# A turn ahead of the values: the order of TensorE's work in a head of attention

## The chip, the cores and the metric

One core of a Trainium2 chip runs one program. The time is the device's, in microseconds (us), from three runs of the kernel; lower is better. The profile is one further execution.

## What is computed

Two layers on `x` of 4 batches, 512 rows and 256 columns. Each layer is a cross attention with 16 heads of width 16 and a feed-forward part, each added to `x` through a gate. The attention of the first layer, cut to what matters (the second has one mask for all heads in place of the bias for each):

```python
q = split_heads(query @ Wq.T + bq)
k = split_heads(key @ Wk.T + bk)
v = split_heads(value @ Wv.T + bv)
scores = jnp.einsum('bhqd,bhkd->bhqk', q, k) / jnp.sqrt(jnp.asarray(DH, q.dtype))
scores = scores + relative_bias
scores = jnp.where(key_padding_mask[:, None, None, :], scores, -jnp.inf)
attn = jax.nn.softmax(scores, axis=-1)
out = jnp.einsum('bhqk,bhkd->bhqd', attn, v)
```

The first layer's feed-forward part is an expert network chosen for each batch, the second's a mixture of eight experts with a shared one.

## The kernel before, in words

Each engine has its own instruction stream, written out by hand, and waits on semaphores. A layer's attention is one phase, `attention_phase`. It runs over 4 groups of heads (`hg`), in each over 4 batches (`b`), in each over 4 heads (`j`): 64 heads one after the other, numbered `n`. Below, a "batch" is four heads of one group, 16 of them in a layer.

A head of one batch has scores of 512 x 512, in four tiles of 128 queries by 512 keys. A tile goes through these stations:

- PE, `scores` (L601): one matmul into one of three PSUM banks. Tiles go out in pairs. After the first two heads the tiles of two heads alternate in `order`: (n,0), (n+1,0), (n,1), (n+1,1) and so on. A matmul may start once the tile three places before in the ring of banks has been read.
- DVE, `add_bias` (L686): adds bias or mask, keeps the row's minimum of the negative as `nmax`, writes the tile to SBUF (`s`, or the spare `xT` for every other pair of heads).
- POOL, `subtract_max` (L795), for 7 of 8 tiles, ACT (L740) for the eighth.
- PE, `turn` (L615): 32 transposes of 64 x 64 bring the head's four tiles into four other PSUM banks. It waits until all four tiles of the head are subtracted (`less_max`, `pool_less_max`), and until ACT has read the banks for the head before (`exp0`, `exp1`).
- ACT, `exps` (L745, and L753 in a batch's last head): the exponential, into `pT`.
- PE, `values` (L633): one key tile `kt` of all four heads of a batch; four calls, kt = 0 to 3, make the batch's output. It can start when the last head's exponentials are there. ACT's `keep_out` copies the finished output to `oT`; a batch later PE's `turn_out` (L643) turns it, and DVE divides by the sums.

So the values of a batch are computed during the four heads of the next batch, one call in each head. `scores` runs ahead of `turn` by two heads and more: `tiles_issued(n)` is 10 + 4n tiles (8 for n = 0), and `between(n)` says that head n issues two tiles (`early`) and two more (`late`). Behind a batch's values stands POOL's copy `keep_values` (L801), once a batch, ahead of the last three tiles of its part.

SP loads queries, keys and, in the first layer, a bias of 1 MB for each head. DVE waits for the bias (`bias_loaded`).

In a head PE issues: values, early scores, in a batch's first head the turned output, the turn, late scores. That is the loop `body` of the PE stream.

Of the kernel before, what the change touches and what calls it, by code (L numbers as in the profile page):

```python
# [31 lines left out]
HG = 4  # L32
# [410 lines left out]
def attention_phase(nc, sem, sb, at, dram, bias_dram, zeroed, tag):  # L443
# [28 lines left out]
    def groups(eng, body):  # L472

        for hg in range(GROUPS):
            body(hg, hg == 0, hg == GROUPS - 1)

    def before(hg, b):

        return (hg, b - 1) if b else (hg - 1, B - 1)
# [23 lines left out]
    def between(n):  # L503

        return (0, 6) if n == 0 else (2, 2)
# [23 lines left out]
    def ring_bank(place):  # L529

        return (0, 1, 7)[place % 3]

    def tiles_issued(n):

        return AHEAD + 4 * n + (2 if n else 0)

    def slot(b, j):

        return j + HG * (b % 2) if j < HG - 1 else j

    with nc.Block() as block:
# [44 lines left out]
        @block.tensor  # L586
        def _(pe):
            pe.nop().then_inc(scores_done, 32)

            def scores(u):  # L590

                for n, k in order[u:u + 2]:
                    hg, b, j = n // M, n % M // HG, n % HG
                    place = tile_place[at_order[n, k]]
                    loads = hg * 2 + b // 2 + 1 - (b % 2 if at.joint_load else 0)
                    if j == 0 and k == 0 and loads:
                        pe.wait_ge(qk_loaded[b % 2], loads * (16 * LOADS))
                    if place >= 3:
                        pe.wait_ge(*ring[place - 3])
                    rows = slice(j % 2 * HP, j % 2 * HP + KEPT)  # L600
                    nc.tensor.matmul(sb.ps[:, ring_bank(place), :],  # L601
                                     at.qs[rows, j // 2, b % 2, k * P:(k + 1) * P],
                                     at.ks[rows, j // 2, b % 2, :], start=True, stop=True).then_inc(scores_done, 1)

            def turn(hg, m):

                pe.wait_ge(less_max, act_upto[hg * M + m])
                pe.wait_ge(pool_less_max, pool_upto[hg * M + m])
                for kt in range(QT):
                    if kt % 2 == 0:  # L610
                        pe.wait_ge(exp1 if kt else exp0, hg * M + m + 1)
                    for qt in range(QT):
                        for r in range(2):
                            rows, col = slice(r * HP, (r + 1) * HP), (kt % 2 * QT + qt) * HP
                            last = nc.tensor.transpose(sb.ps[:, 2 + kt // 2 * 2 + r, col:col + HP],  # L615
                                                       at.s[m % 4][rows, qt, kt * P:(kt + 1) * P],
                                                       sb.ident[rows, rows])
                    if kt % 2 == 1:
                        last.then_inc(turned, 1)

            def values(hg, b, kt):

                if kt == 0:
                    pe.wait_ge(exp_first, hg * B + b + 1)
                else:
                    pe.wait_ge(exp1 if kt >= 2 else exp0, hg * M + HG * b + HG + 1)
                if kt == 0:
                    pe.wait_ge(v_ready, hg * B + b + 1)
                    pe.wait_ge(out_kept, hg * B + b + 1)
                for j in range(HG):  # L630
                    pair = at.pT[:, slot(b, j), kt // 2 * 2:kt // 2 * 2 + 2, :].rearrange(
                        "p r (k t s) -> p k t r s", k=2, t=QT)
                    last = nc.tensor.matmul(sb.ps[VW * j:VW * (j + 1), 6, :], at.vq[:, b % 2, kt, j, :],  # L633
                                            pair[:, kt % 2, :, :, :], start=(kt == 0), stop=(kt == QT - 1))
                if kt == QT - 1:
                    last.then_inc(av_done, 1)

            def turn_out(hg, b):
                pe.wait_ge(out_kept, hg * B + b + 2)
                place = out_place[hg * B + b]  # L640
                pe.wait_ge(*ring[place - 3])
                for qt in range(QT):
                    last = nc.tensor.transpose(sb.ps[:, ring_bank(place), qt * P:(qt + 1) * P], at.oT[:, qt * P:(qt + 1) * P],  # L643
                                               sb.ident[:, :])
                last.then_inc(out_turned, 1)

            for u in range(0, AHEAD, 2):
                scores(u)

            def body(hg, first, last):  # L650
                for m in range(M):
                    b, j = m // HG, m % HG
                    u = tiles_issued(hg * M + m)
                    if not (first and b == 0):
                        values(*before(hg, b), j)
                    early, late = between(hg * M + m)
                    for i in range(0, early, 2) if u < len(order) else ():
                        scores(u + i)
                    if j == 0 and not (first and b < 2):
                        turn_out(*before(*before(hg, b)))  # L660
                    turn(hg, m)
                    for i in range(early, early + late, 2) if u + early < len(order) else ():
                        scores(u + i)
                if last:
                    turn_out(hg, B - 2)
                    for kt in range(QT):
                        values(hg, B - 1, kt)
                    turn_out(hg, B - 1)
            groups(pe, body)

        @block.vector
# [1640 lines left out]
```

## Time and profile before

| what | value |
|---|---|
| median of 3 runs | 944.98 us |
| lowest of them | 939.49 us |
| highest of them | 4893.35 us |
| the profiled execution's own time | 940.07 us |
| its span, first to last instruction | 938.3 us |
| mean granted TensorE clock | 0.975 |

The three runs are the first timings of the kernel; the highest stands alone. In the profile, attention takes two stretches of the span, from about 61 to 266 us and from about 415 to 616 us. The profile counts an engine as busy while an instruction that computes runs; the start of an instruction minus the start of the one before is what a step costs on an engine that never idles.

### The profile page before, as it was taken

What the parts mean: (1) busy time and instruction counts of PE and PEld (TensorE: products, weight loads), DVE (VectorE), ACT (ScalarE), POOL (GpSimd) and SP (SyncE); (2) the same over time, 40 slices, a digit from 0 to 9 for tenths busy, and PEclk for the clock granted to TensorE, in tenths of its full rate; (3) what the DMA queues carried; (4) which work ended last, traced back from release to release, by engine and by line L of the source; (5) the groups of instructions that cost most, each with busy time, mean ns of one, the idle gap of its engine ahead of it and who ended that gap; (6) DMA issues with size and microseconds to landing.
All of it is one profiled execution on the core that took longest, in us unless ns stands there. A gap on an engine that the chain in (4) does not pass through costs nothing. (4 is left out here: it accounts for less than half of the span.)

```text
span 938.3 us, 20996 instructions
## 1 busy us (share of the span) xinstructions
PE 895.9 (95%) x7733; PEld 555.0 (59%) x7734; DVE 563.9 (60%) x1659; ACT 452.2 (48%) x645; POOL 459.9 (49%) x648
## 2 busy tenths in 40 slices
PE   7889999999989999999999999997999899999998
PEld 2466555555567455556555555574555677777765
DVE  4558989899828334367999999757522222222226
ACT  2426767788745233346777777833111122323221
POOL 2017878888847600017888888741264022222224
PEclk9987999999999999986999999999999999999999
DMA  9853535453143331344242424033822021212216
GB/s 327 307 207 115 181 113 169 146 165 108 32 144 104 131 111 64 121 146 112 69 123 71 123 69 126 22 94 147 252 86 92 11 68 58 68 57 68 62 60 238
DMA packets 70372, 111.82 MB, mean 119 GB/s; under 512 B 17574, under 2 KB 41578, under 8 KB 68106
## 3 DMA queue, kind: packets, MB, share of 16 engines
q1 hardware_dynamic: 62458, 91.26, 31.6%
q0 software_dynamic: 3408, 9.38, 2.8%
q10 hardware_dynamic: 4416, 9.96, 2.8%
q8 instruction: 58, 0.95, 0.4%
q14 instruction: 32, 0.26, 0.1%
HBM read 76.99 MB, written 33.58 MB: 118 GB/s over the span
## 5 line engine op out<-in xcount | busy, mean ns | idle before, releaser
L745 ACT ACTIVATE pT<-ps 128x1024 f32<-128x1024 f32 x224 | 219.9, 1027 | 86.5 <-PE ps L615 86.4
L795 POOL TENSOR_SCALAR s<-s,nmax 128x512 f32<-128x512 f32 x218 | 148.5, 693 | 171.8 <-DVE nmax L686 168.1
L795 POOL TENSOR_SCALAR xT<-xT,nmax 128x512 f32<-128x512 f32 x224 | 153.2, 694 | 55.5 <-DVE nmax L686 55.4
L686 DVE CUSTOM_DVE_ANT_0 xT<-ps,bias 128x512 f32<-128x512 f32 x240 | 156.3, 688 | 23.8 <-PE ps L601 14.5
L686 DVE CUSTOM_DVE_ANT_0 s<-ps,bias 128x512 f32<-128x512 f32 x224 | 145.8, 688 | 11.8 <-PE ps L601 5.8
L601 PE MATMUL ps<-ks,qs 49*128 49x512 f32 (+1 forms) x512 | 140.8, 511 | 5.9 <-DVE nmax L686 3.1
L633 PE MATMUL ps<-pT,vq 128*32 128x512 f32 x1024 | 137.2, 612 | 2.9
L601 PEld LDWEIGHTS ps<-ks,qs 49*128 49x128 f32 (+1 forms) x512 | 57.6, 199 | 115.4 <-DVE nmax L686 88.2
L1683 POOL DMA_INDIRECT slots_out<-y,id x39 | 37.7, 967 | 140.2 <-DVE y L2019 136.8
L1767 PE MATMUL ps<-gu,xgT 128*128 x312 | 98.9, 460 | 0.7 <-ACT xgT L1851 0.7
L2013 DVE TENSOR_TENSOR hs<-gs,ps 128x352 f32<-128x352 f32 x39 | 20.3, 520 | 105.4 <-ACT gs L1856 105.4
L615 PEld LDWEIGHTS ps<-ident,xT 64*128 64x128 f32 x2048 | 78.8, 144 | 7.7 <-issue 3.4
L615 PE MATMUL ps<-ident,s 64*128 64x64 f32 x2048 | 81.8, 232 | 0.0
L615 PEld LDWEIGHTS ps<-ident,s 64*128 64x128 f32 x2048 | 77.3, 146 | 7.2 <-issue 5.0
L615 PE MATMUL ps<-ident,xT 64*128 64x64 f32 x2048 | 80.1, 229 | 0.0
L1718 PE MATMUL ps<-xT,sgu 128*128 128x512 f32 x176 | 77.1, 594 | 1.9 <-DVE h L1977 1.1
L1767 PEld LDWEIGHTS ps<-gu,xgT 128*128 128x128 f32 x312 | 56.3, 190 | 25.6 <-issue 0.9
L1785 PE MATMUL ps<-dn,hT 128*128 (+1 forms) x234 | 57.1, 380 | 0.7 <-ACT hT L1861 0.7
L1718 PEld LDWEIGHTS ps<-xT,sgu 128*128 128x128 f32 x176 | 33.1, 190 | 41.6 <-issue 38.8
L1845 ACT ACTIVATE g<-ps 128x512 f32<-128x512 f32 (+1 forms) x24 | 14.3, 596 | 83.7 <-PE ps L1718 83.7
L1856 ACT ACTIVATE gs<-ps 128x352 f32<-128x352 f32 x39 | 18.1, 463 | 73.7 <-PE ps L1767 73.7
L1785 PEld LDWEIGHTS ps<-dn,hT 128*128 128x128 f32 (+1 forms) x234 | 41.6, 191 | 5.1 <-issue 0.9
(202 smaller groups left out, 1207.3 us busy)
## 6 DMA issues: line engine op xcount, KB each, us to landing
bias<-in_bias SPq DMA_DIRECT2D x13, 1024.0 KB, 7.6
qs<-qk_scratch SPq DMA_DIRECT2D x180, 64.0 KB, 2.4
ks<-qk_scratch SPq DMA_DIRECT2D x62, 128.0 KB, 2.9
gu<-in_gate_up SPq DMA_DIRECT2D x8, 704.0 KB, 8.8
slots_in<-zeros SPq DMA_DIRECT2D x4, 1280.0 KB, 6.3
xg<-slots_in SPq DMA_DIRECT2D x39, 130.0 KB, 2.1
qk_scratch<-parts ACTq DMA_DIRECT2D x8, 512.0 KB, 5.5
qk_scratch<-parts SPq DMA_DIRECT2D x8, 512.0 KB, 5.0
```

Source lines behind the costliest of these rows:

```text
L601: nc.tensor.matmul(sb.ps[:, ring_bank(place), :], at.qs[rows, j // 2, b % 2, k * P:(k + 1) * P], at.ks[rows, j // 2, b % 2, :], start=True ...
L615: last = nc.tensor.transpose(sb.ps[:, 2 + kt // 2 * 2 + r, col:col + HP], at.s[m % 4][rows, qt, kt * P:(kt + 1) * P], sb.ident[rows, rows])
L633: last = nc.tensor.matmul(sb.ps[VW * j:VW * (j + 1), 6, :], at.vq[:, b % 2, kt, j, :], pair[:, kt % 2, :, :, :], start=(kt == 0), stop=(kt ...
L686: nc.vector.tensor_tensor_reduce(at.s[n % 4][:, k, :], sb.ps[:, ring_bank(tile_place[u]), :], at.bias[bias % BIAS_SLOTS][:, k, :], -1.0, 3 ...
L745: nc.scalar.activation(at.pT[:, slot(m // HG, m % HG), 2 * half:2 * half + 2, :], sb.ps[:, 2 + 2 * half:4 + 2 * half, :], ACT.Exp).then_in ...
L795: nc.gpsimd.tensor_scalar(s, s, -1.0, at.nmax[:, n % 4, k:k + 1], ALU.mult, ALU.add).then_inc(pool_less_max, 1)
L1683: pool.indirect_dma_start(out=scr.ys, out_offset=bass.IndirectOffsetOnAxis(ap=m.id[:, u, 0:1], axis=0), in_=m.y[:, u, :], in_offset=None). ...
L1718: last = nc.tensor.matmul(sb.ps[:, 2 * (k % 2) + g, :], m.sgu[:, c, a:a + P], sb.xT[:, c, b * S:(b + 1) * S], start=(c == 0), stop=(c == D ...
L1767: last = nc.tensor.matmul(sb.ps[:, 2 * (u % 2) + g, 0:I1], m.xgT[:, u % 2, c, :], m.gu[:, bass.ds(e, 1), c, g * I1:(g + 1) * I1].rearrange ...
L1785: last = nc.tensor.matmul(sb.ps[:, 6 + u % 2, 0:D], m.hT[0:n, u % 2, i, :], m.dn[0:n, bass.ds(e, 1), i, :].rearrange("p e f -> p (e f)"), ...
L1856: nc.scalar.activation(m.gs[:, u % 2, :], sb.ps[:, 2 * (u % 2), 0:I1], ACT.Silu).then_inc(silu_done, 1)
L2013: nc.vector.tensor_tensor(m.hs[:, u % 2, 0:I1], m.gs[:, u % 2, :], sb.ps[:, 2 * (u % 2) + 1, 0:I1], ALU.mult).then_inc(prod_done, 1)
```

## The change

In a head of attention, PE now issues the turn first, then the early scores, the turned output, the values, and the late scores. In the last head of a batch the values stay in front, and the turn follows directly, ahead of both pairs of scores. Nothing else is changed: all other engines' streams are the same.

```diff
                     b, j = m // HG, m % HG
                     u = tiles_issued(hg * M + m)
-                    if not (first and b == 0):
+                    waits_for_values = j == HG - 1
+                    if waits_for_values and not (first and b == 0):
                         values(*before(hg, b), j)
+                    turn(hg, m)
                     early, late = between(hg * M + m)
                     for i in range(0, early, 2) if u < len(order) else ():
                         scores(u + i)
                     if j == 0 and not (first and b < 2):
                         turn_out(*before(*before(hg, b)))
-                    turn(hg, m)
+                    if not waits_for_values and not (first and b == 0):
+                        values(*before(hg, b), j)
                     for i in range(early, early + late, 2) if u + early < len(order) else ():
                         scores(u + i)
```

The PE stream before, from the turn of a batch's head 2 over its head 3 into head 0 of the next (L615 is a turn, L601 scores, L633 values, L643 the turned output):

```order
L615 MATMUL ps<-ident,xT 128x64 x32
L601 MATMUL ps<-ks,qs 128x512 x2
L633 MATMUL ps<-pT,vq 32x512 x4
L601 MATMUL ps<-ks,qs 128x512 x2
L615 MATMUL ps<-ident,xT 128x64 x32
L601 MATMUL ps<-ks,qs 128x512 x2
L633 MATMUL ps<-pT,vq 32x512 x4
L601 MATMUL ps<-ks,qs 128x512 x2
L643 MATMUL ps<-ident,oT 128x128 x4
L615 MATMUL ps<-ident,s 128x64 x32
L601 MATMUL ps<-ks,qs 128x512 x2
L633 MATMUL ps<-pT,vq 32x512 x4
```

The same place now:

```order
L615 MATMUL ps<-ident,xT 128x64 x32
L601 MATMUL ps<-ks,qs 128x512 x2
L633 MATMUL ps<-pT,vq 32x512 x4
L601 MATMUL ps<-ks,qs 128x512 x2
L633 MATMUL ps<-pT,vq 32x512 x4
L615 MATMUL ps<-ident,xT 128x64 x32
L601 MATMUL ps<-ks,qs 128x512 x4
L615 MATMUL ps<-ident,s 128x64 x32
L601 MATMUL ps<-ks,qs 128x512 x2
L643 MATMUL ps<-ident,oT 128x128 x4
L633 MATMUL ps<-pT,vq 32x512 x4
L601 MATMUL ps<-ks,qs 128x512 x2
```

Head 3's values and its turn now follow each other, its two pairs of scores stand together behind them, and the next batch's first turn comes right behind those; that batch's first values have gone behind the turned output.

The PE stream before, at the start of a layer, where the count of scores ahead of each turn can be read:

```order
L601 MATMUL ps<-ks,qs 128x512 x8
L615 MATMUL ps<-ident,s 128x64 x32
L601 MATMUL ps<-ks,qs 128x512 x8
L615 MATMUL ps<-ident,s 128x64 x32
L601 MATMUL ps<-ks,qs 128x512 x4
L615 MATMUL ps<-ident,xT 128x64 x32
```

The same place now:

```order
L601 MATMUL ps<-ks,qs 128x512 x8
L615 MATMUL ps<-ident,s 128x64 x32
L601 MATMUL ps<-ks,qs 128x512 x6
L615 MATMUL ps<-ident,s 128x64 x32
L601 MATMUL ps<-ks,qs 128x512 x4
L615 MATMUL ps<-ident,xT 128x64 x32
```

Ahead of the second turn stand 14 tiles instead of 16, and so two fewer ahead of each later one.

## Rows read from the trace of the kernel before

**Rows 1.** Stretches: length; busy us (instructions) of PE, PEld, DVE, ACT, POOL; clock, DMA, GB/s.

```profile
61.00:82.00 21.00, 19.37 (x162) 12.96 (x162) 16.33 (x52) 11.81 (x15) 12.68 (x20) 0.52 0.39 132
520.00:600.00 80.00, 79.26 (x1240) 45.44 (x1235) 74.83 (x233) 64.54 (x83) 67.52 (x103) 1.00 0.37 95
```

**Rows 2.** Timeline of PE, one batch: start, us, line, tiles, count.

```profile
145.19 1.22 PE L615 MATMUL ps<-ident,s 64*128 64x64 f32 x32
...
147.63 0.50 PE L601 MATMUL ps<-ks,qs 49*128 49x512 f32 x2
147.96 1.17 PE L615 MATMUL ps<-ident,s 64*128 64x64 f32 x32
148.94 0.47 PE L601 MATMUL ps<-ks,qs 49*128 49x512 f32 x2
149.34 1.07 PE L633 MATMUL ps<-pT,vq 128*32 128x512 f32 x8
150.34 0.51 PE L601 MATMUL ps<-ks,qs 49*128 49x512 f32 x2
150.68 1.17 PE L615 MATMUL ps<-ident,xT 64*128 64x64 f32 x32
...
153.06 0.51 PE L601 MATMUL ps<-ks,qs 49*128 49x512 f32 x2
153.40 1.17 PE L615 MATMUL ps<-ident,xT 64*128 64x64 f32 x32
154.38 0.47 PE L601 MATMUL ps<-ks,qs 49*128 49x512 f32 x2
154.96 1.07 PE L633 MATMUL ps<-pT,vq 128*32 128x512 f32 x8
155.96 0.50 PE L601 MATMUL ps<-ks,qs 49*128 49x512 f32 x2
156.39 0.66 PE L643 MATMUL ps<-ident,oT 128*128 128x128 f32 x4
156.97 1.22 PE L615 MATMUL ps<-ident,s 64*128 64x64 f32 x32
```

**Rows 3.** Timeline of PE, end of the second layer's attention.

```profile
605.89 1.07 PE L633 MATMUL ps<-pT,vq 128*32 128x512 f32 x8
606.88 1.31 PE L615 MATMUL ps<-ident,xT 64*128 64x64 f32 x32
```

**Rows 4.** Timeline of DVE and POOL, same batch; POOL's copy from its line.

```profile
148.53 2.04 POOL L795 TENSOR_SCALAR xT<-xT,nmax 128x512 f32<-128x512 f32 x3
150.06 0.69 DVE L686 CUSTOM_DVE_ANT_0 s<-ps,bias 128x512 f32<-128x512 f32 x1
150.85 4.90 POOL L795 TENSOR_SCALAR s<-s,nmax 128x512 f32<-128x512 f32 x7 [0.29 <-DVE nmax L686]
150.88 0.69 DVE L686 CUSTOM_DVE_ANT_0 s<-ps,bias_more 128x512 f32<-128x512 f32 x1
...
L801 POOL COPY vq<-v x32: 391/398/404, 71.7 to 605.0; 128x256 f32<-128x256 f32 x32
```

**Rows 5.** Timeline of PE behind two stalls of the first layer, idle in brackets.

```profile
119.64 0.78 PE L643 MATMUL ps<-ident,oT 128*128 128x128 f32 x4 [2.00 <-DVE nmax L686]
120.36 1.97 PE L615 MATMUL ps<-ident,s 64*128 64x64 f32 x32
...
124.06 0.50 PE L601 MATMUL ps<-ks,qs 49*128 49x512 f32 x2
...
169.15 0.63 PE L643 MATMUL ps<-ident,oT 128*128 128x128 f32 x4 [0.92 <-DVE nmax L686]
169.71 1.22 PE L615 MATMUL ps<-ident,s 64*128 64x64 f32 x32
```

**Rows 6.** Timeline of PE, start of the first layer's attention.

```profile
74.40 2.08 PE L615 MATMUL ps<-ident,xT 64*128 64x64 f32 x29
...
77.87 2.08 PE L615 MATMUL ps<-ident,xT 64*128 64x64 f32 x29
79.66 0.77 PE L601 MATMUL ps<-ks,qs 49*128 49x512 f32 x1
```

## The prediction

> **What bounds the kernel now.** I read the page first, for the shares of the span: TensorE (PE) is by far the busiest engine. A share of the whole span says little of one stage, so the table of stretches came next, for a piece in the middle of the second attention layer: PE 79.26 of 80 us at a granted clock of 1.00, VectorE (DVE) 74.83, GpSimd (POOL) 67.52, ScalarE (ACT) 64.54 [rows 1]. PE sets the pace there, but DVE has 6% and POOL 16% left, so a push on either shows at once.
>
> Then the timeline of PE for one batch of four heads [rows 2]. I write T(j) for the turn of head j, S for a pair of score tiles, V(j) for the values, O for the turn of the output, and count from start to start. T(0) stands at 145.19, T(1) at 147.96, T(2) at 150.68, T(3) at 153.40, the next T(0) at 156.97: 11.78 us a batch. None of these rows carries a wait in front. The steps are T to S 0.98 (147.96 to 148.94), S to V 0.40, V to S 1.00, S to T 0.34, S to O 0.43 and O to what follows 0.58. One row that the change brings everywhere is V directly followed by T; the end of the second layer has it, 605.89 to 606.88, 0.99 [rows 3].
>
> Last, the engines between a score tile and the turn that needs it [rows 4]. DVE starts on a tile 0.54 after its pair started on PE (150.34 to 150.88) and takes 0.69; POOL starts the subtraction 0.10 after DVE's end (150.06 + 0.69 to 150.85) and takes 0.70 (4.90 for seven). So a tile is ready for its turn 0.54 + 0.69 + 0.10 + 0.70 = 2.03 after its pair, if POOL has nothing else to do. POOL also has a copy of 0.40, once a batch, ahead of its last three tiles for head 2.
>
> **The change, part by part.** Nothing is added or removed: only the PE stream changes, so PE's own work costs the same. What moves is the distance between a score pair and the turn that needs it.
>
> The order tables say which pair that is. Ahead of T(n) PE had issued 4n+12 tiles, now 4n+10. Heads go in twos, their tiles alternate, and an even head's last tile is number 4n+7 of the stream, an odd head's 4n+4. For even heads the needed pair was the last but two; now it is the last but one, and it stands directly behind the turn before. Odd heads keep three tiles more and never wait.
>
> *Today's slack.* For T(2) at 150.68 the needed pair is the one at 147.63, 3.05 earlier. POOL's second tile of the group at 148.53 is that head's last; it ends at 148.53 + 2 x 0.70 = 149.93, so 0.75 are to spare. For T(0) at 156.97 the pair is that at 153.06, 3.91 earlier; the sixth of POOL's seven from 150.85 ends at 155.05, so 1.9 are to spare [rows 2, 4].
>
> *After.* Head 2: its pair is issued behind T(1), and only S to V 0.40, V to S 1.00 and S to T 0.34 lie between it and T(2): 1.74 instead of 3.05. That is 1.31 earlier, with 0.75 to spare. Head 0: behind T(3) come two pairs in a row and then T(0). A pair behind a pair isn't in the trace; it costs between nothing and the 0.5 that a pair is busy, so T(0) would stand 0.34 to 0.85 behind its pair, against the 2.03 that the tile needs. Both turns wait. Behind a waiting turn are queued, in PE's order, the next scores, the output's turn and the values: DVE starves meanwhile, its tiles come late, and so does the next turn. The wait feeds itself each batch.
>
> One batch, from T(0):
> - T(0) to T(2). PE alone: 0.98 S 0.43 O 0.58 V 1.00 S, so the second pair starts at 2.99. DVE has its first of the two done at 2.99 + 0.54 + 0.69 = 4.22, POOL starts on it at 4.32 and does this tile, the copy and two more before head 2 is complete: 0.70 + 0.40 + 0.70 + 0.70, to 6.82. Now it is 5.49: +1.33. (PE alone would be there at 6.05. If POOL had no queue, the pair behind T(1), at 3.33 + 0.98, would allow 6.34, or +0.85: that is the lower bound.)
> - T(2) to T(3): no wait; PE does T 0.98 S 0.40 V 1.00 S 0.40 V 0.99 = 3.77, since two values lie in this piece. Now 2.72: +1.05.
> - T(3) to T(0): 0.98 to the needed pair, and 2.03: 3.01. Now 3.57: -0.56. What a pair behind a pair costs is hidden under the 2.03. T(0) also needs the exponentials of head 3; ACT, busy 81% in the stretch, has room in a longer batch, so I cost that at nothing [rows 1].
>
> Sum 13.60, against 11.78: +1.82 a batch. It runs through 14 batches of 16 in each layer (the first has no values, and in the last PE has no more scores to issue, where I take the first term, 1.33, alone). So 28 x 1.82 + 2 x 1.33 = 53.6.
>
> What the change gains is in there: the values of kt 0 wait for the exponentials today, with a step of 0.58 in place of 0.40 (154.38 to 154.96), so 0.17 a batch [rows 2].
>
> *Stalls on the bias.* In the first layer DVE waits for a bias from HBM: PE idles 2.00 before O at 119.64 and 0.92 before O at 169.15 [rows 5]. With batches 1.8 longer the loads land in time; the first stall also cost clock: O to the second S is 4.42 there (119.64 to 124.06) against 0.58 + 2.44 = 3.02 in the batch above (O to T, 145.19 to 147.63), 1.40. Together -4.3.
>
> *The start of each layer.* Its first heads run at 1.2 GHz (granted 0.52 from 61 to 82 us [rows 1]): T to S is 1.79 (77.87 to 79.66) and turns come every 3.47 [rows 6]. The chain to an even head is 1.79 + 0.77 (the S row) + 0.69 + 0.10 + 0.70 = 4.05 there: +0.6 for T(2) and T(4), in two layers +2.3. The first values now come behind T(4) instead of ahead of it, and until then the low clock may stay; I take 1 a layer. Together +4.3, which cancels the gain above.
>
> Total: 940.07 + 53.6 = **994**. The profiled execution is 4.9 under the median of the three runs and within 0.6 of the best.
>
> **The clock.** PE will be idle two times a batch, about 0.8 before T(2) and up to 1.5 around the second pair and T(0). After the idle 2.00 the granted clock fell to 1.2 GHz (T 1.97 at 120.36); after the idle 0.92 it stayed at 2.4 GHz (T 1.22 at 169.71) [rows 5]. The new idle is split by a pair of scores and lies nearer to 0.92, so I leave the clock at full. The Trainium skill, "TensorE: Matmul & The Clock Gate", section "A second HAM failure mode: psum-queue depth-cycling", tells of a kernel whose many short pauses between groups of matmuls kept the clock swinging between its two levels. By that rule this batch would lose clock each time, which is the first rival below.
>
> **Rivals.**
> - *The clock falls in each batch.* For it: two idles a batch, and a stretch from V(3) to the next V(0) in which only turns and scores run, as at the start of a layer, where the clock stayed low [rows 6]. Against it: the row at 169.71. Price: 1.40 a batch, 28 times, 39: 994 + 39 = 1033. Where it decides the rows leave open: an idle of 0.92 kept the clock, one of 2.00 lost it.
> - *The turns are ready anyway, not slower.* The values fill the time for which PE would wait, their wait of 0.17 goes 30 times (5), and the bias stalls are filled by a turn (4): 931. It would need more slack than the moves take: 1.31 at head 2 and over 3 at head 0, with 0.75 and 1.9 measured. It decides where DVE and POOL finish a tile in under 0.9 instead of 2.03.
> - *Only DVE and PE matter*, POOL's queue being empty by then: the lower bound 0.85 for T(2), so +1.34 a batch: 28 x 1.34 + 2 x 0.85 - 4.3 = 35, or 975.
>
> **How the numbers follow.** The forecast with its own bounds, 975 to 1010 (upper end: no gain at the bias, 0.1 more latency at each of 56 waits, 5 more at the two layer starts), has 0.70; the clock rival 0.20; ready anyway 0.06; something else 0.04. The range reaches from 975 to 1035 and so takes in the clock rival. About 2% is what a measurement of this kernel can tell from no change. Forecast and clock rival are slower by over 2% (over 964); ready anyway is within 2%, and so is half of the rest: slower 0.92, same 0.06, faster 0.02.
>
> **What would show it.** In the profile of after: T to T in a batch of 3.3, 3.5, 3.8 and 3.0 in place of 2.8, 2.7, 2.7 and 3.6; PE idle ahead of the turns of even heads, none ahead of odd ones; POOL's last tile of the head ending just before; DVE's busy share in the middle of a layer falling from 94% to about 81%; no wait for a bias. I am wrong if even turns start without idle, if batches last 11.8 or less, or if a turn takes 1.97 in the middle of a layer.

## The result, and the profile after

| | before | after |
|---|---|---|
| median | 944.4 us | 999.45 us (998.49 to 1002.26) |
| ratio to before, 95% interval | | 1.062 [1.059, 1.065] |
| profiled execution | 940.07 us | 1002.26 us |
| its span, mean granted clock | 938.3 us, 0.975 | 1000.5 us, 0.969 |

The change makes the kernel 6.2% slower; 994 had been forecast. One disturbed run of before (4893.35) is left out of the ratio. The experiments below are compared with 17 runs of before taken beside them, whose median was 941.59 us for the lead of ten, the late copy, the values behind and the even order, and 942.71 us for the others.

The table of stretches of after, the same stretch of time as in [rows 1], again in the middle of the second layer (columns as there):

```profile
520.00:600.00 80.00, 71.58 (x1044) 39.08 (x1044) 64.10 (x201) 55.21 (x68) 57.60 (x89) 1.00 0.34 88
```

PE has gone from 79.26 to 71.58 of 80 us and DVE from 74.83 to 64.10. No engine is full any more: PE, DVE and POOL wait for one another in a ring, as the rows below show. The clock is at its higher level (granted 1.00), as before.

The timeline of PE in after, from the turn of a batch's head 3 over the next batch to its head 3; these rows answer to [rows 2]. Behind the PE stream the lines of after stand three further down than in before: L689 is `add_bias`, L798 `subtract_max`, L804 `keep_values`, L756 the exponentials of a batch's last head, L762 `keep_out`. The other runs shift by a few lines more or less.

```profile
163.13 1.22 PE L615 MATMUL ps<-ident,xT 64*128 64x64 f32 x32
164.16 0.71 PE L601 MATMUL ps<-ks,qs 49*128 49x512 f32 x3
165.42 0.49 PE L601 MATMUL ps<-ks,qs 49*128 49x512 f32 x1 [0.56 <-DVE nmax L689]
166.26 1.22 PE L615 MATMUL ps<-ident,s 64*128 64x64 f32 x32 [0.35 <-issue]
167.26 0.50 PE L601 MATMUL ps<-ks,qs 49*128 49x512 f32 x2
167.69 0.66 PE L643 MATMUL ps<-ident,oT 128*128 128x128 f32 x4
168.28 1.07 PE L633 MATMUL ps<-pT,vq 128*32 128x512 f32 x8
169.28 0.50 PE L601 MATMUL ps<-ks,qs 49*128 49x512 f32 x2
169.61 1.17 PE L615 MATMUL ps<-ident,s 64*128 64x64 f32 x32
170.59 0.48 PE L601 MATMUL ps<-ks,qs 49*128 49x512 f32 x2
...
171.99 0.50 PE L601 MATMUL ps<-ks,qs 49*128 49x512 f32 x2
173.08 1.22 PE L615 MATMUL ps<-ident,xT 64*128 64x64 f32 x32 [0.60 <-issue]
...
175.94 1.06 PE L633 MATMUL ps<-pT,vq 128*32 128x512 f32 x8
176.94 1.22 PE L615 MATMUL ps<-ident,xT 64*128 64x64 f32 x32
```

T(0) stands at 166.26, T(1) at 169.61, T(2) at 173.08, T(3) at 176.94: 3.35, 3.47, 3.86, and 3.13 from T(3) at 163.13 to T(0). There is idle before T(0) and T(2), none before T(1) and T(3). One more wait stands before the fourth of the score tiles that are issued in head 3 (0.56): it needs the bank of a tile that DVE has yet to read.

What the two turns waited for is not in the brackets ("issue" says only that the profile shows no releaser). The timeline of DVE and POOL in after, the same batch, shows it:

```profile
164.67 0.69 DVE L689 CUSTOM_DVE_ANT_0 s<-ps,bias_more 128x512 f32<-128x512 f32 x1 [1.12 <-PE ps L601]
165.47 1.37 POOL L798 TENSOR_SCALAR s<-s,nmax 128x512 f32<-128x512 f32 x2 [1.06 <-DVE nmax L689]
...
170.60 0.69 POOL L798 TENSOR_SCALAR xT<-xT,nmax 128x512 f32<-128x512 f32 x1 [0.66 <-DVE nmax L689]
171.24 0.40 POOL L804 COPY vq<-v 128x256 f32<-128x256 f32 x1
171.62 2.04 POOL L798 TENSOR_SCALAR xT<-xT,nmax 128x512 f32<-128x512 f32 x3
```

Before T(0): scores at 164.16, DVE at 164.67, POOL at 165.47; the first of its two tiles, the last one of head 0, ends at 165.47 + 0.69 = 166.16, and T(0) starts at 166.26, 2.10 behind its scores. Before T(2): POOL runs without a gap from 170.60, a tile, the copy, and three tiles; the second of the three, the last one of head 2, ends at 171.62 + 1.36 = 172.98, and T(2) starts at 173.08. DVE itself was kept waiting by PE, 1.12 before its tile at 164.67.

### The profile page after: what moved, and what is told of

It reads as the page before. It is cut to its first block and busy times, and to the rows that moved or that the text cites. A ratio compares the mean times of both kernels' runs of the same rounds, so it can differ in the third digit from the quotient of the medians.

```text
span 1000.5 us, 20996 instructions
## 1 busy us (share of the span) xinstructions
PE 919.3 (92%) x7733; PEld 559.4 (56%) x7734; DVE 563.1 (56%) x1659; ACT 459.2 (46%) x645; POOL 460.7 (46%) x648
## 5 line engine op out<-in xcount | busy, mean ns | idle before, releaser
L798 POOL TENSOR_SCALAR s<-s,nmax 128x512 f32<-128x512 f32 x218 | 149.2, 694 | 224.3 <-DVE nmax L689 221.9
L798 POOL TENSOR_SCALAR xT<-xT,nmax 128x512 f32<-128x512 f32 x224 | 153.3, 694 | 61.5 <-DVE nmax L689 61.5
L689 DVE CUSTOM_DVE_ANT_0 s<-ps,bias 128x512 f32<-128x512 f32 x224 | 146.4, 689 | 58.1 <-PE ps L601 52.0
L689 DVE CUSTOM_DVE_ANT_0 xT<-ps,bias 128x512 f32<-128x512 f32 x240 | 156.1, 688 | 28.7 <-PE ps L601 25.3
L601 PE MATMUL ps<-ks,qs 49*128 49x512 f32 (+1 forms) x512 | 148.3, 507 | 22.3 <-DVE nmax L689 19.4
L633 PE MATMUL ps<-pT,vq 128*32 128x512 f32 x1024 | 138.2, 618 | 0.0
L601 PEld LDWEIGHTS ps<-ks,qs 49*128 49x128 f32 (+1 forms) x512 | 61.6, 202 | 120.4 <-DVE nmax L689 90.1
L615 PEld LDWEIGHTS ps<-ident,xT 64*128 64x128 f32 x2048 | 73.9, 144 | 54.5 <-issue 30.9
L615 PE MATMUL ps<-ident,xT 64*128 64x64 f32 x2048 | 81.9, 231 | 18.6 <-issue 18.5
L615 PE MATMUL ps<-ident,s 64*128 64x64 f32 x2048 | 82.7, 233 | 9.7 <-issue 9.6
L615 PEld LDWEIGHTS ps<-ident,s 64*128 64x128 f32 x2048 | 78.8, 147 | 20.9 <-issue 19.1
L1848 ACT ACTIVATE g<-ps 128x512 f32<-128x512 f32 (+1 forms) x24 | 14.3, 596 | 83.7 <-PE ps L1721 83.7
```

Of the source, the lines that this page charges most:

```text
L601: nc.tensor.matmul(sb.ps[:, ring_bank(place), :], at.qs[rows, j // 2, b % 2, k * P:(k + 1) * P], at.ks[rows, j // 2, b % 2, :], start=True ...
L689: nc.vector.tensor_tensor_reduce(at.s[n % 4][:, k, :], sb.ps[:, ring_bank(tile_place[u]), :], at.bias[bias % BIAS_SLOTS][:, k, :], -1.0, 3 ...
L798: nc.gpsimd.tensor_scalar(s, s, -1.0, at.nmax[:, n % 4, k:k + 1], ALU.mult, ALU.add).then_inc(pool_less_max, 1)
```

## The experiments

The theory (A) is that the turns of heads 0 and 2 wait because PE now issues two score tiles fewer ahead of each turn. The number of tiles issued ahead of a turn is called its lead below: 4n+12 before, 4n+10 after. The rivals: the new order costs as such, or the clock does. A second part of A came up when the first runs were planned: where two pairs of scores stand together, the second has to wait for the three banks.

Below are the distances between the starts of turns, for a batch in the middle of the second layer, in us:

| kernel | T(0)-T(1) | T(1)-T(2) | T(2)-T(3) | T(3)-T(0) | batch | median |
|---|---|---|---|---|---|---|
| before | 2.77 | 2.72 | 2.72 | 3.57 | 11.78 | 942 to 944 |
| after | 3.35 | 3.47 | 3.85 | 3.13 | 13.81 | 999.45 |
| lead of ten | 3.71 | 2.72 | 3.81 | 2.40 | 12.63 | 963.82 |
| copy late | 3.35 | 3.13 | 3.86 | 3.13 | 13.47 | 991.13 |
| values behind | 3.54 | 3.71 | 4.09 | 3.50 | 14.83 | 1030.2 |
| even, second layer | 3.54 | 2.72 | 2.72 | 2.72 | 11.70 | 947.35 |
| even, last head put back | 3.54 | 2.72 | 2.72 | 2.72 | 11.70 | 942.86 |
| last head only | 2.77 | 2.72 | 2.38 | 4.78 | 12.65 | 962.46 |
| first heads only | 3.68 | 3.48 | 4.19 | 1.93 | 13.28 | 982.22 |
| all heads turn first | 3.67 | 2.72 | 2.72 | 4.24 | 13.34 | 994.19 (one execution) |

**Lead of ten.** The changed kernel with its lead given back.

```diff
-    AHEAD = 8
+    AHEAD = 10
```

> The changed kernel with AHEAD = 10 instead of 8: the order within a head stays as changed, but ahead of each turn stand 4n+12 score tiles again, as before the change. In the changed kernel a batch of four heads lasts 13.81 us, from turn to turn 3.35, 3.47, 3.85, 3.13; before it lasted 11.78. Theory A (the turns of heads 0 and 2 wait because their tiles went out two tiles later): the wait before T(2) goes (3.47 to 2.72, which is what PE alone needs), and before T(0) only the ring of three banks is left: 0.98 from the turn to the scores, 0.54 + 0.69 until the first tile is read, 0.34 to the turn, 2.55 in place of 3.13. Batch 3.35 + 2.72 + 3.85 + 2.55 = 12.47, so 28 x -1.34 = -37: about 962 us. Rival B (the new order itself costs it, by instructions standing next to each other or by the clock, and not the lead): batch stays at 13.8, about 999. Rival C (the lead is all of the loss): batch 11.8, about 944.

Measured: 963.82 us, ratio to before 1.023 [1.018, 1.028]. The timeline of PE, around the place where after waits for T(0) and T(2):

```profile
508.89 0.71 PE L601 MATMUL ps<-ks,qs 48*128 48x512 f32 x3
510.16 0.49 PE L601 MATMUL ps<-ks,qs 48*128 48x512 f32 x1 [0.56 <-DVE nmax L689]
510.26 1.21 PE L615 MATMUL ps<-ident,s 64*128 64x64 f32 x29
...
516.35 0.51 PE L601 MATMUL ps<-ks,qs 48*128 48x512 f32 x2
516.68 1.17 PE L615 MATMUL ps<-ident,xT 64*128 64x64 f32 x32
```

Both turns follow their scores without a wait; the wait of 0.56 for the bank is still there. So the order stands, the lead is back, and 1.18 of the 2.03 per batch are gone: A holds for that part, and B and C, which put the whole loss on one side, fall. The batch is 12.63 and not 12.47, since T(0) to T(1) takes 3.71 where 3.35 was expected; T(3) to T(0) is a little shorter, 2.40 for 2.55. The rest of the loss, 0.85, is not the lead.

**Copy late.** After, with POOL's copy moved.

```diff
-                    if m % HG == 1:
+                    if m % HG == HG - 1:
                         keep_values(hg, m // HG)
```

> The changed kernel with GpSimd's copy of the values moved from head 1 of a batch to head 3 (nothing else). Theory A with a queue on POOL: the copy of 0.40 us lies in the chain from the second pair of scores to the last tile of head 2, so T(1) to T(2) falls from 3.47 to 3.07, the batch from 13.81 to 13.41, 28 x -0.40 = -11: about 988 us. Rival (POOL's queue is not in the chain, the lower bound of the prediction, or something else waits there): no difference, 999.

Measured: 991.13 us, 1.052 [1.047, 1.057]; T(1) to T(2) 3.13 for 3.47 and the other distances as in after. The timeline of PE and POOL, from T(1) to T(2); the third of POOL's tiles is the last one of head 2:

```profile
529.83 1.17 PE L615 MATMUL ps<-ident,s 64*128 64x64 f32 x32
530.82 2.71 POOL L798 TENSOR_SCALAR xT<-xT,nmax 128x512 f32<-128x512 f32 x4 [0.67 <-DVE nmax L689]
532.95 1.22 PE L615 MATMUL ps<-ident,xT 64*128 64x64 f32 x32 [0.25 <-issue]
```

An instruction of 0.40 on an engine that is busy 72% of the time (57.60 of 80) was worth 0.34 a batch: POOL's queue is in the chain, and the third rival of the prediction (POOL's queue empty, 975) falls.

**Values behind the turn, lead kept.** From the kernel before: the values move, the lead stays.

```diff
-                    if not (first and b == 0):
+                    if j == HG - 1 and not (first and b == 0):
                         values(*before(hg, b), j)
...
                     turn(hg, m)
+                    if j < HG - 1 and not (first and b == 0):
+                        values(*before(hg, b), j)
```

> The order before (early scores ahead of the turn, so 4n+12 tiles ahead of each turn as before), with only the values moved behind the turn in heads 0 to 2, ahead of the late scores. If the lead alone made the loss, this is as fast as before: 11.6 to 11.8 us a batch, 939 to 945 us. If the even spacing of the score pairs counts as well (three banks, DVE reads a tile in 0.62), then late pair and early pair of the next head now stand together and the second has to wait until the first is read: T to V 0.98, V to S 1.00, S to S 0.54 + 0.69, S to T 0.34 = 3.55 in three heads, about 3.4 to 3.7 in head 3: batch 14.0 to 14.3, 28 x 2.3 to 2.5 = 64 to 70 over before: 1004 to 1015 us.

Measured: 1030.2 us, 1.093 [1.087, 1.098], the slowest of all. The timeline of PE around one head:

```profile
557.81 1.07 PE L633 MATMUL ps<-pT,vq 128*32 128x512 f32 x8
558.81 0.73 PE L601 MATMUL ps<-ks,qs 48*128 48x512 f32 x3
560.09 0.50 PE L601 MATMUL ps<-ks,qs 48*128 48x512 f32 x1 [0.56 <-DVE nmax L688]
560.20 1.40 PE L615 MATMUL ps<-ident,s 64*128 64x64 f32 x32
561.52 1.07 PE L633 MATMUL ps<-pT,vq 128*32 128x512 f32 x8
```

Here the turn keeps its lead and never waits, but in three places of a batch two pairs of scores stand together, and the fourth tile stands 1.27 or 1.28 behind the first (ahead of T(3) the values of the batch before still stand between the pairs). Keeping the lead is not enough for the old speed: 3.05 a batch are lost here. The size was missed: 14.83 a batch where at most 14.3 was expected. T(1) to T(2) took 3.71 and T(2) to T(3) 4.09 where 3.55 was put in. From a turn to the values it took 1.32 (560.20 to 561.52) in place of 0.98, for a reason that no row shows, so how much of the 3.05 is bunching stays open here; the next run shows its price alone. The second layer's first batch with values took 21.15, at the low clock (granted 0.62 from 476 to 497 us), where the first layer's took 16.85.

**The two parts of the change alone.** First the last head, from the kernel before:

```diff
+                    if j == HG - 1:
+                        turn(hg, m)
                     early, late = between(hg * M + m)
...
-                    turn(hg, m)
+                    if j < HG - 1:
+                        turn(hg, m)
```

> The kernel before with the change in the last head of a batch alone: there values, turn, early scores, late scores; heads 0 to 2 as before. Every turn of heads 0 and 2 keeps the tiles that it had ahead of it before. Theory A with its second part (two pairs of scores next to each other cost the time until the first is read from its bank): T(2) to T(3) 0.98 + 0.40 + 0.99 = 2.37; T(3) to T(0) 0.98 to the first pair, 0.54 + 0.69 to the second, 0.40 to the values, 1.00, 0.43, 0.58 = 4.62; batch 2.77 + 2.72 + 2.37 + 4.62 = 12.48, 28 x 0.70 = 20 over before: about 961 us. Rival (only the lead of the turns counts, bunching is free): T(3) to T(0) 3.9, batch 11.8, 941.

Measured: 962.46 us, 1.018 [1.013, 1.023], batch 12.65; A had put 961, the rival 941. The timeline of PE:

```profile
530.65 1.07 PE L633 MATMUL ps<-pT,vq 128*32 128x512 f32 x8
531.65 1.22 PE L615 MATMUL ps<-ident,xT 64*128 64x64 f32 x32
532.68 0.71 PE L601 MATMUL ps<-ks,qs 48*128 48x512 f32 x3
533.95 0.50 PE L601 MATMUL ps<-ks,qs 48*128 48x512 f32 x1 [0.56 <-DVE nmax L689]
534.38 1.06 PE L633 MATMUL ps<-pT,vq 128*32 128x512 f32 x8
```

No turn waits here, and the bunched scores of one head cost 0.87 a batch. That is about what was left of the loss in the run with the lead of ten (0.85). So, with the lead given back first, 1.18 of the loss of after is the lead's and 0.85 the bunching's; the next run shows that this split depends on what is put back first.

Then heads 0 to 2, from the changed kernel:

```diff
-                    turn(hg, m)
+                    if not waits_for_values:
+                        turn(hg, m)
                     early, late = between(hg * M + m)
...
-                    if not waits_for_values and not (first and b == 0):
+                    if waits_for_values:
+                        turn(hg, m)
+                    elif not (first and b == 0):
                         values(*before(hg, b), j)
```

> The changed kernel with the last head of a batch put back as it was: values, early scores, turn, late scores there; heads 0 to 2 as changed. Theory A: T(0) to T(1) 3.35 or up to 3.7 if the output's turn waits for a bank as it does with the lead of ten, T(1) to T(2) 3.47 (POOL's chain as in the changed kernel), T(2) to T(3) 0.98 + 0.40 + 1.00 + 0.40 + 1.00 + 0.34 = 4.12 without a wait, T(3) to T(0): its tiles went out one step ahead of T(3), so 2.03 - 0.34 = 1.7 to 1.85 with POOL's queue; batch 12.6 to 13.15, 28 x 0.9 to 1.4: 962 to 976 us. Rival (most of the loss comes from heads 0 to 2 by their order, whatever the last head does): 13.5 or more, 990 and up.

Measured: 982.22 us, 1.041 [1.037, 1.046], between the two ranges, so neither had it (batch 13.28, where A had at most 13.15). T(1) to T(2) is 3.48 as in after. What was not expected is the releaser before T(0):

```profile
505.86 1.54 PE L615 MATMUL ps<-ident,s 64*128 64x64 f32 x32 [0.48 <-ACT pT L759]
```

T(0) comes so soon behind T(3), 1.93, that it waits for ACT to read the banks, not for POOL. The parts alone cost 1.50 and 0.87 and together 2.03. Put back first, the last head takes only 0.53 off the loss of after: there the wait for the bank is hidden under the wait of T(0) for POOL. With a ring of waits the costs of two edits do not add.

**All heads turn first.** After with AHEAD = 10 and `waits_for_values = False`: evenly spaced scores and the old lead, in both layers. It was executed once, so its time has no interval.

> The changed kernel with AHEAD = 10 and without the exception: the turn first in the last head of a batch too. The scores are then evenly spaced in all heads and the lead is restored, so by these two alone it would be 11.7 a batch, 940 us. Theory A adds why the exception is there: with seven slots the exponentials of the last head share one, so ACT copies the output (after the values of kt 3) ahead of them; the values now stand behind T(3) and a pair of scores, so the next T(0) waits for exponentials that start at 0.98 + 0.40 + 1.06 + 0.48 = 2.9 after T(3) and take 0.95 to its first half: T(3) to T(0) about 3.9 to 4.1 where 2.72 would do; batch 13.0 to 13.3, 975 to 983 us.

Measured: 994.19 us, batch 13.34. The timeline of ACT and PE at the end of a batch:

```profile
595.23 0.60 ACT L762 ACTIVATE oT<-ps 128x512 f32<-128x512 f32 x1 [1.98 <-PE ps L633]
595.72 1.08 ACT L756 ACTIVATE pT<-ps 128x512 f32<-128x512 f32 x2
596.95 1.54 PE L615 MATMUL ps<-ident,s 64*128 64x64 f32 x32 [1.35 <-ACT pT L756]
```

T(3) to T(0) is 4.24, a little more than the theory said (3.9 to 4.1), by the wait that it named: the exponentials wait for the copy of the output, that for the values. This is what the change's exception for the last head avoids, at the price of the bunching. The time is 11 over the range; 9 of that is the clock, which fell in six of the batches: there T(0) to T(1) took 5.16 to 5.20 in place of 3.67, 1.5 each.

**The even order in the second layer.** Without either cost, where there is room for an eighth slot: the kernel before, with this in the second layer (`EVEN`), besides AHEAD = 10, `slot` with eight places, and `keep_out` of a batch in head 0 of the batch after next.

```diff
+                    if EVEN:
+                        turn(hg, m)
                     early, late = between(hg * M + m)
...
+                    if EVEN and not (first and b == 0):
+                        values(*before(hg, b), j)
```

> The kernel before, with the second layer's attention alone in this order: in all four heads turn, early scores, (turned output), values, late scores, so turns, scores, values and scores alternate; AHEAD = 10 there so that each turn keeps its lead; an eighth slot for the exponentials of that layer (the first layer has no room for one), so that the last head's need not wait for the values before, and ACT's copy of the output one head later. Theory A (lead and even spacing are what counts; the order as such costs nothing, and the 0.17 us for which the values of kt 0 wait is gained): T to T 3.33 and three times 2.72, 11.5 to 11.6 a batch in the second layer in place of 11.78, 14 x -0.2 = -3 us, some of it lost at the layer's start: 937 to 941 beside 940. Rival B (a turn in front of the scores costs as such): the second layer's batches get longer than 11.78, by up to half of the change's loss, 940 to 970.

Measured: 947.35 us, 1.006 [1.003, 1.008], so slower by a little. But a batch takes 11.70 for 11.78: with the lead and the spacing kept, and an eighth slot, turn first costs nothing in a batch, and rival B falls. The hoped-for 0.2 to 0.3 did not come: T(0) to T(1) is 3.54 and not 3.33, since the turned output waits for a bank.

```profile
522.81 0.47 PE L602 MATMUL ps<-ks,qs 48*128 48x512 f32 x2
523.48 0.63 PE L644 MATMUL ps<-ident,oT 128*128 128x128 f32 x4 [0.20 <-DVE nmax L692]
```

14 times 0.08 is 1.1; the end of the layer lost more: from the last scores to the last values it took 11.60 for 9.45.

The last head of the layer put back:

> The kernel before with the second layer in the even order (as in the run with that order alone), and its last head put back: there the values stand ahead of the turn and ACT copies the output before the exponentials. In the run without this the batches of the second layer were 11.70 in place of 11.78, but from the last scores to the last values it took 11.6 in place of 9.4. This takes those 2.2 back: 939 to 943 beside 941, within what can be measured. If the even order costs elsewhere, it stays at 945 to 947.

Measured: 942.86 us, 0.999 [0.997, 1.002]: no difference to before. In the trace the end of the layer takes 10.31, so 1.3 of the 2.15 came back; why the median fell by more, 4.5, is not shown. No version here beats the kernel before by more than can be measured. The first layer with eight slots was not tried.

## Why the prediction was right, step by step

- *The slack and which turns wait*: right. Of the turns, T(0) and T(2) alone have idle before them, 0.35 and 0.60, each starts 0.10 behind the end of POOL's last tile, and a lead of ten takes both waits away.
- *T(0) to T(2)*: 6.82 forecast, 3.35 + 3.47 = 6.82 measured. The queue on POOL with its copy was in the sum; moving the copy took 0.34 off. That the hundredths agree is luck: from POOL's start to the end of head 2's last tile it took 2.38 (170.60 to 172.98) where 2.50 was put in, and the 0.10 from there to the turn was left out.
- *T(2) to T(3)*: 3.77 forecast, 3.85 measured. *T(3) to T(0)*: 3.01 forecast, 3.13 measured (T(3) reaches its scores after 1.03, not 0.98, and T(0) stands 2.10 behind its pair, not 2.03: again the 0.10 from POOL to the turn was left out). That the exponentials cost nothing here was right too; where T(0) comes sooner, as with the first heads only, it waits for them. The batch came out at 13.81, not 13.60: 28 x 0.21 = 6.
- *A pair behind a pair costs nothing*: right only because the other wait is longer. In the last head only, where no turn waits, the same spot costs 0.87. The prediction nowhere put in the three banks as a cost of their own; for a version that keeps the lead and bunches the scores it would have been too low.
- *The last batch of a layer*: mis-sized. T(0) to T(3) there rose by 2.7 (2.77 + 2.09 + 2.24 before, 3.35 + 3.47 + 3.01 after, first layer), not by 1.33: before has no scores left behind T(1) there (T(1) to T(2) 2.09), while after issues its last pair there and T(2) waits as in every batch (3.47); and T(2) to T(3) holds two values here as well.
- *The bias*: right in kind, -5.0 and not -4.3. DVE has no wait for a bias left in after. But before had a third one, which the prediction overlooked; T(3) to T(0) is 4.11 there and not 3.57. Its row, of DVE:

```profile
215.99 0.69 DVE L686 CUSTOM_DVE_ANT_0 xT<-ps,bias 128x512 f32<-128x512 f32 x1 [0.43 <-DMA bias<-in_bias]
```

- *The start of a layer*: mis-sized. T(1) to T(2) rose by 0.7, about as forecast, but in the first layer T(0) to T(1) fell from 5.90 to 4.68 and T(3) to T(4) from 5.02 to 4.20, and then T(4) to T(5), still at the low clock, rose from 2.71 to 4.74. Over the first two batches it evened out (3.8 more in both layers together, where 2 x 2.03 is counted below), while 4.3 on top was put in.
- *The clock*: left at full, and nearly so; no turn in the middle of a layer took 1.97. The rows at the one place in the first layer where it fell:

```profile
221.50 1.18 PE L615 MATMUL ps<-ident,s 64*128 64x64 f32 x31 [0.34 <-issue]
...
222.94 1.04 PE L643 MATMUL ps<-ident,oT 128*128 128x128 f32 x4
223.90 1.94 PE L633 MATMUL ps<-pT,vq 128*32 128x512 f32 x8
```

The values take 1.94 in place of 1.07, at 1.2 GHz (granted 0.53 from 222.9 to 225.8 us). That batch, and the last one of the second layer, had T(0) to T(1) at 4.87 and 4.88, 1.5 more, so 3 in all where the rival asked for 39. The Trainium skill, "TensorE: Matmul & The Clock Gate", section "A second HAM failure mode: psum-queue depth-cycling", describes such swings. The traces agree only in part: two falls in the 28 batches behind the starts of after, and six in the run with all heads turning first, where PE idled 1.35 before each T(0).

Together: 940.07 + 28 x 2.03 + 2 x 2.7 - 5.0 + 3 = 1000.3, for 1002.26 in the profiled execution; the other 2.0 lie ahead of the first turn (0.5) and behind the last (1.5). The forecast of 994 came this close partly by luck: the 4.3 put in for the starts, which did not come, made up for most of the 6 that the batches lacked.

## What to carry to other kernels

Moving work ahead of a consumer's inputs costs lead, and lead is counted in tiles on the way through the other engines: compare how long the needed tile takes (2.1 here) with what now stands between its issue and its use. Work that feeds a short ring of banks has to stay evenly spaced; bunching it costs even where its consumer never waits (0.87 a batch in the last head only). And an instruction on an engine with 28% of its time free can still be in the chain.

## What was not expected

- The waits for the tiles, for the banks and for the exponentials meet in one ring, so costs do not add: 1.50 and 0.87 alone, 2.03 together.
- With the same idle in every batch of after (0.56 and 0.35 before T(0), 0.60 before T(2)), the granted clock fell in 2 of the 28 batches behind the starts and not in the others. What tells them apart no run here shows.
